# A graph attention on one Trainium2 core: who adds the fourth row of each group

## The chip, the cores and the metric

The kernel runs on one NeuronCore of a Trainium2 chip, as one launch. The metric is the device time of that launch in microseconds, the median of several runs. Everything is float32 here unless said otherwise. Five engines work side by side, each with its own instruction queue: TensorE (PE in the profile) multiplies matrices into PSUM, VectorE (DVE) and ScalarE (ACT) compute elementwise, GpSimd (POOL) issues the gathers, and SyncE (SP) issues plain transfers. They meet through semaphores.

## The reference, cut to what matters

The graph has 1250 nodes of 768 features and 20000 edges. Two graph attentions (GATv2) follow each other, then a relational graph convolution. The second attention has one head and is where the change lies:

```
fs = h @ Wos + bos
fd = h @ Wod + bod
e = leaky_relu(fs[src] + fd[dst], 0.2)        # one row of 768 per edge
logits = sum(e * attn)                         # one number per edge
alpha = softmax of logits over the edges with the same dst
out[dst] = sum over edges of alpha * fs[src]
out = elu(out)
```

The leaky rectifier is split as 0.2 x + 0.8 max(x, 0). The part 0.2 x is linear, so its dot product with attn is worked out once per node and travels as column 768 of the rows of fs and fd. Per edge there remains max(fs + fd, 0) times 0.8 attn, summed over the 768 features.

## The kernel before, in words

Nodes are sorted by their number of edges and put into 10 tiles of 128, one node per partition. A **group** is S = 4 edges of each node of a tile: 4 rows of 776 numbers in each partition. A table says which tile each group belongs to. There are 48 groups, run as a hardware loop of 12 turns with U = 4 groups unrolled in each. The sums are kept in a running softmax: top holds the largest logit so far, den the sum of exponentials, acc the weighted sum of rows, and with every group the old sums are scaled by exp(old top - new top).

The second attention is the function attention_single, from L1110. Who does what for group u:

- **GpSimd** (gather_edges, L790 to L798): copies the place of the node's next record into index, adds one, gathers the record of group u+3 (rec), then gathers the four rows of group u+2 with four indirect transfers. It waits for the sums (summed) of the group that used the row buffer before, and for VectorE's signal read.
- **TensorE**: first the add for group u+2: for each half of 384 columns it multiplies the fourth row (BY_PE = 3) by the identity and then fd by the identity into the same PSUM tile pS (L1201, L1203). Then the weighted sums of group u: four matmuls of two halves with diagonal matrices share as weights, into pA (L1219), and last the old sum acc with share 0 (L1224), once ScalarE has stored acc of the group before (kept). One float32 matmul shows as two records, so a group has 8 records of add, 16 of L1219 and 4 of L1224.
- **VectorE**, for group u: arguments (L1275 to L1287, ten small steps to ex), count (L1292 to L1297), dot of group u+1, weigh (L1303 to L1307). The dot adds fd to rows 0 to 2 into leak (L1253), adds the linear parts (lin, L1256), and runs four multiply-and-sum instructions max(x, 0) * attr with an accumulated sum (L1266): three on leak and the fourth on pS, for which it waits on sum_pe. Before the loop there is the dot of group 0, so 49 dots run, the last of them for a spare group.
- **ScalarE**: exp of ex (L1181), five diagonal matrices share from the identity (L1185), and the copy of pA back to acc for the group before (keep, L1172).

The order on each engine is written out by hand in the program. Nothing is planned by costs. Waits between engines have a slack of one or two groups: the PSUM tiles, dots, lin, ex and share are double, the row buffers fourfold. At the end of the stage all engines meet at a barrier.

Of the kernel before, what the change touches and what calls it, by code (L numbers as in the profile page):

```python
# [4 lines left out]
F32, I32, BF16 = mybir.dt.float32, mybir.dt.int32, mybir.dt.bfloat16  # L5
# [6 lines left out]
P = 128  # L12
# [7 lines left out]
HALF = D // 2  # L20
ROWS_AHEAD = 2
S = 4
U = 4
# [44 lines left out]
def gnn_kernel(nc, io, out):  # L68
    ctx = ExitStack()
    with ctx:  # L70
        taken = {}

        def fresh(name):

            taken[name] = taken.get(name, 0) + 1
            return name if taken[name] == 1 else f"{name}_{taken[name]}"

        def sb(name, shape, dt, where=ctx):
            return where.enter_context(nc.sbuf_tensor(fresh(name), shape, dt))

        def pb(name, shape, dt, where):
            return where.enter_context(nc.psum_tensor(fresh(name), shape, dt))
# [17 lines left out]
        ident = sb("ident", [P, P], F32)  # L100
# [16 lines left out]
        def sems(where, *names):  # L117
            made = [nc.alloc_semaphore(fresh(n)) for n in names]
            where.semaphores += made
            return made  # L120

        @contextmanager
        def stage():

            with ExitStack() as st:
                st.semaphores = []
                yield st
                nc.clear_and_free_semaphores(st.semaphores)
                nc.all_engine_barrier()
# [358 lines left out]
        fdt = sb("fdt", [P, NT + 1, W], F32, fd_ctx)  # L488
# [3 lines left out]
        HB = [(0, 0, HALF), (1, HALF, D)]  # L492

        def halves(psum, rows=P):

            return psum[0:rows, :, 0:HALF]

        def split(ap):
            return ap.rearrange("p (a b) -> p a b", a=2)
# [62 lines left out]
        with stage() as st:  # L562
# [3 lines left out]
            of = [[sb(f"of{w}{b}", [P, W], F32, st) for b in range(2)] for w in range(2)]  # L566
            wt = [sb(f"wt{w}", [P, KC, D], F32, st) for w in range(2)]
            bias = [sb(f"bias{w}", [P, D], F32, st) for w in range(2)]
            attr = sb("attr", [P, D], F32, st)
# [173 lines left out]
        def sum_tiles(eng, tile_from, count, i):  # L743

            tiles = []
            for lo in range(0, count, PACK):
                packed = eng.value_load(tile_of_group[0:1, ds(i * U + (tile_from + TBACK + lo), 1)], min_val=0,
                                        max_val=(1 << 4 * PACK) - 1)
                for k in range(min(PACK, count - lo)):
                    tiles.append(eng.snap((packed >> (4 * k)) & 15).with_bounds(min_val=0, max_val=NT))  # L750
            return tiles
# [91 lines left out]
        def rows_wait(eng, b, i, off):  # L843

            eng.wait_ge(b["row_in"][off % U], i * (16 * S) + 16 * S * (off // U + 1))
# [263 lines left out]

        def attention_single():  # L1110

            BY_PE = S - 1
            with stage() as st:
                b = slot_buffers(st, W)
                row, val = b["row"], b["val"]
# [5 lines left out]
                attr = sb("attr", [P, D], F32, st)  # L1121
                leak = sb("leak", [P, S, D], F32, st)
# [8 lines left out]
                share = [sb(f"share{u}", [P, S + 1, P], F32, st) for u in range(2)]  # L1131
                dsum = sb("dsum", [P, 1], F32, st)
                pA = [pb(f"pA{u}", [P, 2, 512], F32, st) for u in range(2)]
                pS = [pb(f"pS{u}", [P, 2, 512], F32, st) for u in range(2)]
                att_in, dve_step, init_ok = sems(st, "att_in", "dve_step", "init_ok")
                sum_ok = Signal(st, "sum_ok", BY_PE, U, U)
                sum_pe = Signal(st, "sum_pe", 1, U, U)
                logits = Signal(st, "logits", S, U, U)
                lin_ok = Signal(st, "lin_ok", 1, U, U)
                ex_in = Signal(st, "ex_in", 1, U, U)  # L1140
# [2 lines left out]
                summed = Signal(st, "summed", 1, U, U)  # L1143
                total = Signal(st, "total", 1, U, U)
# [4 lines left out]
                def of(ap, tile):  # L1149
                    return ap[:, tile, :] if isinstance(tile, int) else ap[:, ds(tile, 1)].rearrange("p o f -> p (o f)")  # L1150

                with nc.Block() as block:
                    @block.sync
                    def _(sp):
                        sp.dma_start(attr[:], io["L0_gnn_attno"].rearrange("h d -> (h d)").partition_broadcast(P))\
                          .then_inc(att_in, 16)
                        sp.wait_ge(att_in, 16)
# [32 lines left out]

                    @block.tensor
                    def _(pe):
                        for s in (summed, total, sum_pe):
                            s.open(pe)
                        pe.wait_ge(init_ok, 1)

                        def add(i, off, tile):
                            rows_wait(pe, b, i, off)
                            logits.wait(pe, i, off - 2)
                            for q, lo, up in HB:  # L1200
                                pe.matmul(pS[off % 2][:, q, 0:HALF], ident[:], row[off % U][:, BY_PE, lo:up],  # L1201
                                          start=True, stop=False)
                                last = pe.matmul(pS[off % 2][:, q, 0:HALF], ident[:], of(fdt, tile)[:, lo:up],  # L1203
                                                 start=False, stop=True)
                            last.then_inc(sum_pe.sem, 1)

                        add(0, 0, 0)
                        second, = sum_tiles(pe, 1, 1, 0)
                        add(0, 1, second)
                        turns = pe.value_load(ctl[0:1, C_TURNS:C_TURNS + 1], min_val=1, max_val=MAX_TURNS)  # L1210
                        with pe.Fori(0, turns) as i:
                            t = sum_tiles(pe, 0, U + 2, i)
                            for u in range(U):
                                add(i, u + 2, t[u + 2])
                                shared.wait(pe, i, u)
                                kept.wait(pe, i, u - 2)
                                for j in range(S):
                                    for q, lo, up in HB:
                                        last = pe.matmul(pA[u % 2][:, q, 0:HALF], share[u % 2][:, 1 + j, :], row[u][:, j, lo:up],  # L1219
                                                         start=j == 0, stop=False)  # L1220
                                last.then_inc(summed.sem, 1)
                                kept.wait(pe, i, u - 1)
                                for q, lo, up in HB:
                                    last = pe.matmul(pA[u % 2][:, q, 0:HALF], share[u % 2][:, 0, :], of(acc, t[u])[:, lo:up],  # L1224
                                                     start=False, stop=True)
                                last.then_inc(total.sem, 1)

                    @block.vector
                    def _(dve):
# [18 lines left out]
                        def dot(i, off, tile):  # L1248
                            rows_wait(dve, b, i, off)
                            fd = of(fdt, tile)  # L1250
                            for j in range(BY_PE):
                                logits.wait(dve, i, off - 1, j + 1)
                                dve.tensor_tensor(leak[:, j, :], row[off % U][:, j, 0:D], fd[:, 0:D], ALU.add)\  # L1253
                                   .then_inc(sum_ok.sem, 1)
                            lin_ok.wait(dve, i, off - 1)
                            dve.tensor_tensor(lin[off % 2][:], row[off % U][:, :, D:W][:, :, 0],  # L1256
                                              fd[:, D:D + 1].to_broadcast([P, S]), ALU.add).then_inc(lin_ok.sem, 1)
                            for j in range(S):
                                if j < BY_PE:
                                    sum_ok.wait(dve, i, off, j + 1)  # L1260
                                    ins = dict(out=leak[:, j, :], in0=leak[:, j, :], in1=attr[:])
                                else:
                                    logits.wait(dve, i, off - 1, j + 1)
                                    sum_pe.wait(dve, i, off)
                                    ins = dict(out=split(leak[:, j, :]), in0=halves(pS[off % 2]), in1=split(attr[:]))
                                dve.scalar_tensor_tensor(scalar=0.0, op0=ALU.max, op1=ALU.mult, **ins,  # L1266
                                                         accum_out=dots[off % 2][:, j, :]).then_inc(logits.sem, 1)

# [43 lines left out]
                        with dve.Fori(0, turns) as i:  # L1312
                            t = sum_tiles(dve, 0, U + 1, i)
# [331 lines left out]

        settle(True)
        attention_single()
        settle(False)

# [221 lines left out]
        with stage() as st:  # L1871
            b = slot_buffers(st, D)
# [276 lines left out]
```

## Time and profile before

| | us |
|---|---|
| median of 3 runs | 3903.91 |
| lowest and highest of them | 3902.19, 3904.19 |
| the profiled execution, its time | 3898.73 |
| the profiled execution, its span | 3897.1 |
| second attention in it, first to last work | 1262 to 1762 |

The profile is of one execution of its own. Its span runs from the first to the last instruction, and 1.6 us of its time lie around it. In the rows, PE is the matmul part of TensorE and PEld its loads of weights; PEclk is the share of the full clock granted to TensorE, where 0.50 is 1.2 GHz and 1.00 is 2.4 GHz. Ends of matmuls are modelled, so the records overlap. An idle time is followed by what ended it; "issue" is time for which the profile shows no releaser. L with a number is a line of the program.

### The profile page before, as it was taken

How to read it: one execution, taken by the hardware profiler on the slowest of the kernel's cores; microseconds unless marked ns; L12 is line 12 of the kernel's file. 1: busy time of each engine (PE TensorE's matmuls, PEld its weight loads, DVE VectorE, ACT ScalarE, POOL GpSimd, SP SyncE). 2: the span in 40 equal slices, each digit the busy share in tenths (PEclk: the TensorE clock that was granted, in tenths of full speed). 3: DMA queues.
4: the chain of work that ended last, by engine and by line, in shares of the span. 5: the costliest groups of instructions: out<-in, count | busy, mean ns of one | idle time of the engine just before them, and what ended most of it. 6: DMA issues, size and time to landing. Idle time of an engine off the chain costs nothing. (4 is left out here: it accounts for less than half of the span.)

```text
span 3897.1 us, 63629 instructions
## 1 busy us (share of the span) xinstructions
PE 3095.4 (79%) x14356; PEld 2355.9 (60%) x14357; DVE 2506.5 (64%) x5040; ACT 1734.7 (45%) x5380; POOL 1494.4 (38%) x1783
## 2 busy tenths in 40 slices
PE   0196788888697999994779999999999964444699
PEld 0053444444354555552369999999999964444455
DVE  8233889898666888885645554455545549999412
ACT  0010788888621222222324444444444428888400
POOL 0373545454355666661111111111111137777200
PEclk9998899999898999997889999999999986666799
DMA  0233444343454555552155555555555545555300
GB/s 26 79 86 107 136 127 129 117 128 118 147 182 141 163 155 158 157 154 81 44 187 186 180 177 180 183 182 179 176 186 182 184 134 170 176 174 174 128 9 32
DMA packets 181911, 546.64 MB, mean 140 GB/s; under 512 B 37415, under 2 KB 82299, under 8 KB 181563
## 3 DMA queue, kind: packets, MB, share of 16 engines
q0 software_dynamic: 77264, 331.42, 27.7%
q1 hardware_dynamic: 53772, 143.14, 11.9%
q10 hardware_dynamic: 50832, 71.59, 5.1%
q8 instruction: 17, 0.28, 0.0%
q14 instruction: 26, 0.21, 0.0%
HBM read 428.42 MB, written 117.91 MB: 140 GB/s over the span
## 5 line engine op out<-in xcount | busy, mean ns | idle before, releaser
L1804 PE MATMUL pO<-wh,gT 128*128 128x384 f32 x4128 | 1094.5, 339 | 4.5 <-DVE wl L1842 4.5
L1804 PEld LDWEIGHTS pO<-wh,gT 128*128 128x128 f32 x4128 | 750.7, 188 | 5.3 <-DVE wl L1842 5.3
L1804 PE MATMUL pO<-wl,gT 128*128 128x384 f32 x2064 | 691.8, 335 | 0.0
L798 POOL DMA_INDIRECT row<-fs_d,rec x400 | 439.6, 1099 | 351.4 <-PE pA L986 187.7
L1828 DVE TENSOR_SCALAR cntge<-pT 128x768 int32<-128x768 int32 x173 | 165.7, 958 | 571.2 <-PE pT L504 570.3
L511 PE MATMUL pO<-wt,hT 128*128 128x384 f32 (+1 forms) x1200 | 420.0, 512 | 42.5 <-ACT hT L1510 19.6
L1756 ACT ACTIVATE gT<-cntge 128x256 fp32r<-128x256 f32 x1038 | 371.7, 410 | 170.5 <-PE pO L1804 121.4
L1766 ACT ACTIVATE nrow<-pO 128x384 f32<-128x384 f32 x344 | 165.9, 482 | 542.1 <-PE pO L1804 542.1
L1804 PEld LDWEIGHTS pO<-wl,gT 128*128 128x128 f32 x2064 | 389.1, 189 | 0.0
L1936 PE MATMUL pC<-identb,own 128*128 128x128 bf16 x960 | 192.9, 304 | 235.0 <-ACT cntge L1917 121.2
L511 PEld LDWEIGHTS pO<-wt,hT 128*128 128x128 f32 (+1 forms) x1200 | 236.8, 200 | 215.9 <-issue 68.7
L924 ACT ACTIVATE sj<-sj 128x96 f32<-128x96 f32 x1176 | 313.1, 268 | 99.7 <-DVE sj L1041 99.7
L1726 POOL DMA_INDIRECT g<-hr_d,gindex x173 | 167.5, 968 | 379.0 <-PE pT L504 373.3
L963 PE MATMUL pS<-row,ident 128*128 128x384 f32 x400 | 184.1, 545 | 128.3 <-DVE sj L1041 89.5
L1737 POOL COPY gindex<-source 128x1 int32 x172 | 43.5, 253 | 614.0 <-DMA g<-hr_d,gindex 614.0
L1936 PEld LDWEIGHTS pC<-identb,own 128*128 128x128 bf16 x960 | 114.2, 143 | 245.4 <-issue 75.6
L1219 PE MATMUL pA<-row,share 128*128 128x384 f32 x768 | 255.8, 486 | 0.0
L986 PE MATMUL pA<-row,ident 128*128 128x384 f32 x768 | 255.5, 486 | 0.0
L798 POOL DMA_INDIRECT row<-y_d,rec x200 | 211.2, 1056 | 66.6 <-issue 61.3
L1914 ACT ACTIVATE far<-nrow,source 128x1280 bf16<-128x1280 f32 x144 | 196.2, 1362 | 83.2 <-DVEq L1989 80.1
L924 ACT ACTIVATION_READ_ACCUMULATOR sj<-sj 128x1 f32 x1176 | 219.7, 187 | 0.0
L1219 PEld LDWEIGHTS pA<-row,share 128*128 128x128 f32 x768 | 146.4, 191 | 102.6 <-issue 1.5
(336 smaller groups left out, 5689.8 us busy)
## 6 DMA issues: line engine op xcount, KB each, us to landing
raw<-in_L_gnn_W_rel_dram SPq DMA_DIRECT2D x204, 384.0 KB
y_d<-nrow ACTq DMA_DIRECT2D x344, 192.0 KB
y_d<-nothing SPq DMA_DIRECT2D x53, 384.0 KB
row<-fs_d,rec POOLq DMA_INDIRECT x400, 4.5
kept_d<-fdt ACTq DMA_DIRECT2D x1, 3840.0 KB, 15.7
kept<-kept_d SPq DMA_DIRECT2D x1, 3840.0 KB
fs_d<-of SPq DMA_DIRECT2D x9, 388.0 KB
fd_d<-of SPq DMA_DIRECT2D x9, 388.0 KB, 2.6
```

Source lines behind the costliest of these rows:

```text
L511: last = pe.matmul(dst[0:rows, q, 0:HALF], rows_t[:, c * P:c * P + rows], w[:, c, lo:up], start=c == 0, stop=c == KC - 1)
L798: pool.indirect_dma_start(b["row"][u][:, j, :], None, table, bass.IndirectOffsetOnAxis(ap=b["rec"][u][:, 2 * j + field:2 * j + field + 1], ...
L924: last = act.activation(of_head, of_head, ACT.Copy, accum_out=dots[off % U][:, j, h:h + 1])
L963: pe.matmul(pS[j][:, q, 0:HALF], ident[:], row[off % U][:, S // 2 + j, lo:up], start=True, stop=False)
L986: last = pe.matmul(pA[:, q, 0:HALF], share, row[u][:, j, lo:up], start=j == 0, stop=j == S - 1)
L1219: last = pe.matmul(pA[u % 2][:, q, 0:HALF], share[u % 2][:, 1 + j, :], row[u][:, j, lo:up], start=j == 0, stop=False)
L1726: pool.indirect_dma_start(g[:], None, hr_d, bass.IndirectOffsetOnAxis(ap=gindex[:], axis=0))\
L1756: act.activation(gT[:, c].bitcast(F32R), cut[:, :, c * P:(c + 1) * P], ACT.Copy).then_inc(gT_ok.sem, 1)
L1766: act.activation(y[:, lo:up], pO[:, q, 0:HALF], ACT.Copy).then_inc(evac_ok.sem, 1)
L1804: last = pe.matmul(pO[:, q, 0:HALF], gT[:, c, half, :].bitcast(F32R), w[:, c, lo:up].bitcast(F32R), start=c == 0 and k == 0, stop=c == KC ...
L1914: act.activation(far[:], of_node[:], ACT.Square, bias=source[u % 2][:, j:j + 1], scale=-1.0)\
L1936: last = pe.matmul(pC[u % 2][:, c // 4, (c % 4) * P:(c % 4 + 1) * P], equal[u % 2][j][:, c * P:(c + 1) * P], identb[:], start=j == 0, stop ...
```

## The change

VectorE adds fd to all four rows of a group. TensorE's add, its PSUM tiles pS and the signal sum_pe are gone. TensorE keeps the weighted sums and the scaled old sum. The fourth multiply-and-sum of VectorE now reads leak, as the other three do.

```diff
--- before.py
+++ after.py
@@ -1109,7 +1109,6 @@
 
         def attention_single():
 
-            BY_PE = S - 1
             with stage() as st:
                 b = slot_buffers(st, W)
                 row, val = b["row"], b["val"]
@@ -1131,10 +1130,8 @@
                 share = [sb(f"share{u}", [P, S + 1, P], F32, st) for u in range(2)]
                 dsum = sb("dsum", [P, 1], F32, st)
                 pA = [pb(f"pA{u}", [P, 2, 512], F32, st) for u in range(2)]
-                pS = [pb(f"pS{u}", [P, 2, 512], F32, st) for u in range(2)]
                 att_in, dve_step, init_ok = sems(st, "att_in", "dve_step", "init_ok")
-                sum_ok = Signal(st, "sum_ok", BY_PE, U, U)
-                sum_pe = Signal(st, "sum_pe", 1, U, U)
+                sum_ok = Signal(st, "sum_ok", S, U, U)
                 logits = Signal(st, "logits", S, U, U)
                 lin_ok = Signal(st, "lin_ok", 1, U, U)
                 ex_in = Signal(st, "ex_in", 1, U, U)
@@ -1190,28 +1187,15 @@
 
                     @block.tensor
                     def _(pe):
-                        for s in (summed, total, sum_pe):
+                        for s in (summed, total):
                             s.open(pe)
                         pe.wait_ge(init_ok, 1)
 
-                        def add(i, off, tile):
-                            rows_wait(pe, b, i, off)
-                            logits.wait(pe, i, off - 2)
-                            for q, lo, up in HB:
-                                pe.matmul(pS[off % 2][:, q, 0:HALF], ident[:], row[off % U][:, BY_PE, lo:up],
-                                          start=True, stop=False)
-                                last = pe.matmul(pS[off % 2][:, q, 0:HALF], ident[:], of(fdt, tile)[:, lo:up],
-                                                 start=False, stop=True)
-                            last.then_inc(sum_pe.sem, 1)
-
-                        add(0, 0, 0)
-                        second, = sum_tiles(pe, 1, 1, 0)
-                        add(0, 1, second)
                         turns = pe.value_load(ctl[0:1, C_TURNS:C_TURNS + 1], min_val=1, max_val=MAX_TURNS)
                         with pe.Fori(0, turns) as i:
-                            t = sum_tiles(pe, 0, U + 2, i)
+                            t = sum_tiles(pe, 0, U, i)
                             for u in range(U):
-                                add(i, u + 2, t[u + 2])
+                                rows_wait(pe, b, i, u)
                                 shared.wait(pe, i, u)
                                 kept.wait(pe, i, u - 2)
                                 for j in range(S):
@@ -1248,7 +1232,7 @@
                         def dot(i, off, tile):
                             rows_wait(dve, b, i, off)
                             fd = of(fdt, tile)
-                            for j in range(BY_PE):
+                            for j in range(S):
                                 logits.wait(dve, i, off - 1, j + 1)
                                 dve.tensor_tensor(leak[:, j, :], row[off % U][:, j, 0:D], fd[:, 0:D], ALU.add)\
                                    .then_inc(sum_ok.sem, 1)
@@ -1256,13 +1240,8 @@
                             dve.tensor_tensor(lin[off % 2][:], row[off % U][:, :, D:W][:, :, 0],
                                               fd[:, D:D + 1].to_broadcast([P, S]), ALU.add).then_inc(lin_ok.sem, 1)
                             for j in range(S):
-                                if j < BY_PE:
-                                    sum_ok.wait(dve, i, off, j + 1)
-                                    ins = dict(out=leak[:, j, :], in0=leak[:, j, :], in1=attr[:])
-                                else:
-                                    logits.wait(dve, i, off - 1, j + 1)
-                                    sum_pe.wait(dve, i, off)
-                                    ins = dict(out=split(leak[:, j, :]), in0=halves(pS[off % 2]), in1=split(attr[:]))
+                                sum_ok.wait(dve, i, off, j + 1)
+                                ins = dict(out=leak[:, j, :], in0=leak[:, j, :], in1=attr[:])
                                 dve.scalar_tensor_tensor(scalar=0.0, op0=ALU.max, op1=ALU.mult, **ins,
                                                          accum_out=dots[off % 2][:, j, :]).then_inc(logits.sem, 1)
```

## Rows read from the trace of the kernel before

**Rows 1.** The page: busy us (share of the span) xinstructions of each engine.
```profile
PE 3095.4 (79%) x14356; PEld 2355.9 (60%) x14357; DVE 2506.5 (64%) x5040; ACT 1734.7 (45%) x5380; POOL 1494.4 (38%) x1783
```

**Rows 2.** Windows, the stage: PE, PEld, DVE, ACT, POOL busy (x), PEclk, DMA, GB/s.
```profile
1262.00:1762.00 500.00, 461.07 (x1360) 261.27 (x1360) 427.88 (x1357) 137.87 (x349) 317.96 (x338) 0.97 0.51 156
```

**Rows 3.** Timeline, two groups: start us, us, engine, line, op [idle before <-releaser].
```profile
1502.21 0.23 DVE L1275 TENSOR_SCALAR val<-slot,left 128x4 f32<-128x4 f32 x1 [0.15 <-issue]
...
1504.65 0.18 POOL L790 COPY index<-next 128x1 int32 x1 [1.37 <-DVEq L1293]
...
1505.28 2.69 DVE L1253 TENSOR_TENSOR leak<-row,fdt 128x768 f32<-128x768 f32 x3 [0.15 <-issue]
...
1507.89 0.16 DVE L1256 TENSOR_TENSOR lin<-row,fdt 128x4 f32<-128x4 f32 x1
...
1509.09 1.52 POOL L798 DMA_INDIRECT row<-fs_d,rec  x1 [0.30 <-issue]
...
1509.72 0.95 DVE L1266 SCALAR_TENSOR_TENSOR leak<-leak,attr 128x768 f32<-128x768 f32 x1
1509.79 5.32 PE L1219 MATMUL pA<-row,share 128*128 128x384 f32 x16
...
1510.60 0.95 DVE L1266 SCALAR_TENSOR_TENSOR leak<-pS,attr 128x768 f32<-128x768 f32 x1
...
1512.17 0.94 POOL L798 DMA_INDIRECT row<-fs_d,rec  x1 [0.30 <-issue]
1513.40 0.23 DVE L1275 TENSOR_SCALAR val<-slot,left 128x4 f32<-128x4 f32 x1 [1.51 <-issue]
...
1523.24 0.23 DVE L1275 TENSOR_SCALAR val<-slot,left 128x4 f32<-128x4 f32 x1 [0.15 <-issue]
```

**Rows 4.** Waits of VectorE in the stage: us in total, times, longest us.
```profile
DVE val L1275 <- issue: 21.0, 39, 1.6
DVE ge L1295 <- DVE place_f L1292: 7.1, 46, 0.2
```

**Rows 5.** TensorE's waits; lines L1201, L1203, L798: count, duration ns min/median/max, starts.
```profile
PE pS L1201 <- DMA row<-fs_d,rec: 31.4, 33, 2.5
...
L1201 PE MATMUL pS<-row,ident x200: 486/486/1009, 1262.4 to 1753.2; 128*128 128x384 f32 x100
...
L1203 PE MATMUL pS<-fdt,ident x200: 486/486/848, 1263.9 to 1753.8; 128*128 x98, 128*128 128x384 f32 x2
...
L798 POOL DMA_INDIRECT row<-fs_d,rec x178: 942/948/1686, 1290.3 to 1735.7; - x178
```

**Rows 6.** Tile leak: operation, count, duration ns min/median/max, first and last start.
```profile
L1253 DVE TENSOR_TENSOR leak<-row,fdt x147: 948/951/960, 1262.5 to 1750.1; 128x768 f32<-128x768 f32 x147
...
L1266 DVE SCALAR_TENSOR_TENSOR leak<-pS,attr x49: 946/951/953, 1267.9 to 1753.7; 128x768 f32<-128x768 f32 x49
```

**Rows 7.** Timeline of the stage's end.
```profile
1747.41 1.57 ACT L1185 ACTIVATE share<-ident,pe 128x128 f32<-128x128 f32 x5
...
1753.82 5.03 PEld L1219 LDWEIGHTS pA<-row,share 128*128 128x128 f32 x16
...
1754.83 0.16 DVE L1307 TENSOR_TENSOR den<-den,dsum 128x1 f32 x1
...
1760.95 0.81 ACT L1172 ACTIVATE acc<-pA 128x768 f32 x1 [8.85 <-PE pA L1224]
```

**Rows 8.** Timeline of TensorE in the first attention, after an idle gap.
```profile
754.78 1.48 PE L963 MATMUL pS<-row,ident 128*128 128x384 f32 x2 [2.02 <-DVE sj L1041]
756.05 1.49 PE L965 MATMUL pS<-fdt,ident 128*128 x2
...
758.51 0.81 PE L965 MATMUL pS<-fdt,ident 128*128 x2
```

**Rows 9.** Late in the kernel: a gap (timeline), a burst between gaps (windows).
```profile
3331.21 0.39 PE L1936 MATMUL pC<-identb,own 128*128 128x128 bf16 x2 [5.27 <-ACT cntge L1917]
...
3313.00:3318.00 5.00, 4.45 (x40) 4.18 (x40) 4.33 (x13) 4.04 (x4) 3.82 (x4) 0.50 0.52 147
```

## Prediction

> **What bounds the kernel now.** The page comes first, to see that no engine is full over the whole span: TensorE is busy for 79% of it and VectorE for 64% [rows 1]. That says nothing about this change, because it touches one stage of many. The view of windows, cut to the second attention (its first TensorE and VectorE work begins at 1262, its last ScalarE copy ends at 1762), gives 461 us of TensorE and 428 us of VectorE in 500 us, at a granted clock of 0.97 [rows 2]. Both look nearly full, so busy shares cannot tell which sets the pace. TensorE's share is also modelled, since pipelined matmuls overlap.
>
> The timeline of two groups tells more [rows 3]. VectorE goes from one group's first instruction to the next in 9.84 us, or 11.19 us where a turn of four groups ends (1502.21, 1513.40, 1523.24). Inside a group it runs three adds, the small lin, four multiply-and-sum instructions and the small softmax steps, with gaps of 0.15 us. The long gap, 1.51 us, stands only where the loop turns.
>
> Who ends VectorE's idle time is in the view of waits: its largest entry is 21.0 us in 39 pieces put down to issue, the next is a wait on VectorE's own result, the smaller ones are of these two kinds, and no entry names TensorE [rows 4]. TensorE does wait: 31.4 us in 33 pieces for gathered rows, always at the identity matmul of the add [rows 5]. I read this as: **VectorE sets the pace, TensorE has a little room.** The add for group u+2 was issued two groups ahead, so its result always lies ready: in the timeline the multiply-and-sum on pS starts 0.88 us after the one before it, as the others do [rows 3].
>
> **The change, part by part.**
>
> *Added on VectorE.* One more row add per group. There are 147 of three per dot, so 49 dots (48 groups and one spare at the end), each lasting 951 ns in the median [rows 6]. Lasting is not pitch: three adds take from 1505.28 to 1507.89, when the next instruction starts, 0.87 us each [rows 3]. I take 0.875, halfway to the 0.88 pitch of the multiply-and-sum. That is 48 x 0.875 = 42.0 us before the last group's softmax arguments are ready, and 49 x 0.875 = 42.9 us for VectorE's own end. All of it lies on the path, since VectorE has nothing but its own order in front of it. The bounds are 0.87 (41.8 us for 48) and the whole duration 0.951 (45.6 us).
>
> *Moved source.* The fourth multiply-and-sum reads leak from SBUF and no longer pS from PSUM: the one on pS lasts 951 ns in the median [rows 6], the one on leak 0.95 us in the timeline, both with a pitch of 0.88 [rows 3], so nothing. The Trainium skill ("VectorE: DVE Perf Modes", section on the errata that SBUF sources pay a fixed extra latency) gives 58 cycles of fixed cost to an SBUF source and 120 to a PSUM source at 0.96 GHz, which would make this step 65 ns cheaper, 3.2 us over 49; the sum by it would be 34.9 us where mine is 38. The trace does not show that difference, and I follow the trace.
>
> *Waits.* The added add waits for the fourth logit of the group before, which VectorE finished itself long ago; the wait on sum_pe goes. Behind both stand only VectorE's own instructions. Nothing.
>
> *Removed on TensorE.* 200 + 200 records of matmul (pS from row and from fdt), eight per group [rows 5]. At the pitch of 5.32 us for 16, or about 0.324 [rows 3], that is 2.6 us per group. TensorE is not the pace setter, so it gains nothing inside the loop. Its wait for rows of group u+2 goes too; the wait that it gets instead, for rows of group u, is long met, because VectorE's dot of that group already needed them.
>
> *Gained at the end.* Now the shares of the last group are ready at 1747.41 + 1.57 = 1748.98, but TensorE first finishes older work and makes one more useless add, and loads the first share at 1753.82. From there to the last copy of acc it is 7.94 us (1761.76) [rows 7]. Afterwards TensorE stands idle when the shares come: 1748.98 + 42.0 + 0.1 + 7.9 = 1799.0. VectorE's own end, 1754.83 + 0.16 + 42.9 = 1797.9, comes earlier. So the stage ends 37.2 us later, not 42.9.
>
> *GpSimd.* Its row gathers take 0.94 us beside small VectorE work (at 1512.17) and 1.52 us beside wide VectorE work on SBUF (at 1509.09) [rows 3]. VectorE gets 1.75 us more of such work per group, so two gathers may become slow, +1.1 us. From index to the end of the fourth gather is 8.5 us now (1504.65 to 1512.17 + 0.94), so 9.6 afterwards, in a period of 11.0 (the mean of three groups at 9.84 and one at 11.19, plus 0.875). Its rows are needed two dots later. Hidden; if the cover were gone, each microsecond over 11.0 would cost 48 us. The queues of SP and ScalarE get and lose nothing; ScalarE works 137.87 / 48 = 2.9 us per group [rows 2].
>
> *Clock at the end.* The last burst may start at the lower clock (see the rival). Where it fell, about six records ran at the lower pitch of 0.64 before it rose [rows 8], 6 x 0.32 = 1.9 us; I take half, 1 us. The far bound is all 20 records, +6.4 us.
>
> **Sum:** 37.2 + 1 = +38 us on the profiled execution, 3898.7 (span 3897.1 and 1.6 around it) to 3937. The median of the runs shown is 5.2 us above that execution, so 3942.
>
> **Rivals.**
>
> *The clock makes TensorE the bound.* TensorE's group becomes a burst of 20 records, 6.8 us (5.32 and 1.45 as they follow each other), then idle for about 4.2 of 11.0 us. In the first attention the clock had fallen after a gap of 2.02 us: pairs of records took 1.27 us from start to start instead of 0.65, but after 3.7 us of work it was back [rows 8]. Late in the kernel, a gap is 5.27 us and a burst between two gaps has 4.45 us of work at a granted 0.50, the lower clock throughout [rows 9]. If a whole burst stayed there, 20 x 0.64 + 0.6 for the two starts = 13.4 us would exceed the 11.0 of VectorE, and through kept, ex_ok and the gathers everybody would fall in step: 48 x 2.4 = 115 us more, 4057 us. The Trainium skill ("TensorE: Matmul & The Clock Gate", HAM oscillation) states that a loop whose bursts are parted by idle waits goes back to the lower clock and starts every burst cold, which speaks against this change. For the rival: gap as in [rows 9]. Against: a burst longer than that one, and the quick return in [rows 8]; also it limits itself, as a slow burst leaves a short gap. Chance 5%.
>
> *TensorE set the pace already, so the kernel gets faster.* The place is sum_pe and the gathers that wait for summed. VectorE is idle for 493 - 428 = 65 us from 1262 to its end near 1755, 1.35 us per group. If those gaps were really waits on TensorE, they would vanish with its 2.6 us per group, and the added 0.875 would fit: 42.9 - 65 = -22 us, 3882. It decides from 0.875 us of waiting per group on. For it: TensorE's 461 busy us. Against: the gaps are all 0.15 us or at loop turns, and none is ended by TensorE [rows 4]. Chance 2%; a partial case, where about the added time is absorbed (3900 to 3911), 3%.
>
> *GpSimd's gathers become the bound.* If the two fast gathers took the worst 1.69 us instead of 0.95 [rows 5], the chain would be 8.5 + 1.5 = 10.0 us, still under 11.0. Only if the two others and the record's gather grew as well, by 1.5 us together, would it show, 0.5 us per group, 24 us, 3966. For it: one gather in the stage did take 1.69. Against: the median is 0.948. Chance 3%.
>
> **How the numbers follow.** The forecast has the other 87%. Its own range takes the add at 0.87 to 0.951, the end at -3 to +6 us and about 2 us for the run: 3936 to 3953. The other cases hold 13%, so the range that should hold 8 in 10 is this one. A measurement of this kernel can tell some 0.2%, 7.8 us, from no change. Faster by more than that: 2%. Within: 3%. Slower: 95%, the forecast and the two slow rivals.
>
> **What would show it.** Right: 196 adds instead of 147, group to group 10.7 and 12.1 us on VectorE with unchanged gaps, stage about 38 us longer, TensorE's idle time ended by ScalarE's shares, no matmul on pS, and other stages unmoved. The clock in the stage may fall below 0.97 without cost. Wrong: VectorE waits that name ex or rows, groups of 13 us (clock), a VectorE period that stays at 9.84 (TensorE was the bound), or adds longer than 951 ns.

## The result, and the profile after

| | before | changed |
|---|---|---|
| median of 4 runs, us | 3903.05 | 3937.89 |
| lowest and highest | 3900.49, 3904.19 | 3935.66, 3939.36 |
| time and span of the profiled execution | 3898.73, 3897.1 | 3939.36, 3937.7 |
| clock granted to TensorE in it, mean of the span | 0.916 | 0.878 |

The ratio is 1.009 (95% interval 1.0072 to 1.0107), 34.8 us slower by the medians. The forecast was 3942, slower by 38, with a range of 3936 to 3953; the median lies 2 us above the lower end of it.

The view of windows over the stage of the changed kernel (us; busy and count of PE, PEld, DVE, ACT, POOL; PEclk, DMA share, GB/s), which answers to [rows 2]:

```profile
1262.00:1800.00 538.00, 381.39 (x960) 207.33 (x960) 470.11 (x1406) 135.45 (x349) 342.33 (x339) 0.84 0.51 145
```

VectorE is busy for 470 us where it was 428. TensorE is busy for 381 us where it was 461, though its granted clock is down from 0.97 to 0.84. The views of the tiles leak and share and of the gather line (count, duration ns min/median/max, first and last start) answer to [rows 5, 6]:

```profile
L1237 DVE TENSOR_TENSOR leak<-row,fdt x196: 947/951/961, 1262.4 to 1792.9; 128x768 f32<-128x768 f32 x196
L1245 DVE SCALAR_TENSOR_TENSOR leak<-leak,attr x196: 947/951/955, 1266.0 to 1796.4; 128x768 f32<-128x768 f32 x196
...
L1203 PE MATMUL pA<-row,share x768: 486/486/1008, 1275.1 to 1795.9; 128*128 128x384 f32 x192
...
L798 POOL DMA_INDIRECT row<-fs_d,rec x178: 942/1398/1517, 1289.3 to 1776.3; - x178
```

There are 49 more adds (196 instead of 147), each lasting 951 ns as before. All 196 multiply-and-sum instructions read leak now and last 951 ns in the median. The median gather takes 1398 ns instead of 948.

Two groups in the timeline, as [rows 3]:

```profile
1501.32 0.23 DVE L1254 TENSOR_SCALAR val<-slot,left 128x4 f32<-128x4 f32 x1 [0.19 <-issue]
...
1504.30 3.56 DVE L1237 TENSOR_TENSOR leak<-row,fdt 128x768 f32<-128x768 f32 x4
...
1505.04 5.43 PE L1203 MATMUL pA<-row,share 128*128 128x384 f32 x16 [1.19 <-ACT share L1182]
...
1507.78 0.15 DVE L1240 TENSOR_TENSOR lin<-row,fdt 128x4 f32<-128x4 f32 x1
...
1509.93 1.45 POOL L798 DMA_INDIRECT row<-fs_d,rec  x1 [0.30 <-issue]
...
1511.97 0.23 DVE L1254 TENSOR_SCALAR val<-slot,left 128x4 f32<-128x4 f32 x1 [0.19 <-issue]
...
1515.68 7.12 PE L1203 MATMUL pA<-row,share 128*128 128x384 f32 x16 [3.93 <-ACT share L1182]
...
1522.62 0.23 DVE L1254 TENSOR_SCALAR val<-slot,left 128x4 f32<-128x4 f32 x1 [0.19 <-issue]
```

Read VectorE first: 1501.32, 1511.97, 1522.62, so 10.65 us per group; where a turn ends it is 12.04 (to 1534.66). The mean period over the stage is (1787.2 - 1270.0) / 47 = 11.00 us, against (1745.3 - 1269.7) / 47 = 10.12 before, from the first and the last start of val. Four adds take from 1504.30 to 1507.78, 0.87 us each. Only the gap ahead of val is 0.19 us instead of 0.15. Then TensorE: its sums for one group start at 1505.04 after 1.19 us of idleness and take 5.43 us; those for the next start at 1515.68 after 3.93 us of idleness, and the same 16 records take 7.12 us. VectorE's period does not notice. TensorE's timeline shows the longest burst of the stage and one from its middle, then one turn of four groups, as they repeat from 1600 on, and the last two bursts:

```profile
1451.58 8.44 PE L1203 MATMUL pA<-row,share 128*128 128x384 f32 x16 [6.71 <-ACT share L1182]
...
1526.33 5.43 PE L1203 MATMUL pA<-row,share 128*128 128x384 f32 x16 [2.23 <-ACT share L1182]
...
1603.87 7.12 PE L1203 MATMUL pA<-row,share 128*128 128x384 f32 x16 [3.93 <-ACT share L1182]
...
1614.52 7.12 PE L1203 MATMUL pA<-row,share 128*128 128x384 f32 x16 [2.23 <-ACT share L1182]
...
1627.96 7.31 PE L1203 MATMUL pA<-row,share 128*128 128x384 f32 x16 [5.03 <-ACT share L1182]
...
1637.33 5.43 PE L1203 MATMUL pA<-row,share 128*128 128x384 f32 x16 [0.77 <-ACT share L1182]
...
1780.27 7.95 PE L1203 MATMUL pA<-row,share 128*128 128x384 f32 x16 [3.93 <-ACT share L1182]
...
1790.91 5.43 PE L1203 MATMUL pA<-row,share 128*128 128x384 f32 x16 [1.41 <-ACT share L1182]
```

In the turn shown, the bursts after gaps of 2.23, 3.93 and 5.03 us take 7.1 to 7.3 us, three of the four; the one after 0.77, and the last of the stage after 1.41, take 5.43. The gap alone does not decide: the burst at 1526.33 has the same gap of 2.23 as the one at 1614.52 and takes 5.43, not 7.12. Of the stage's 48 bursts 29 take over 5.5 us, and none stays slow to its end: 16 records at the lower pitch of 0.64 would be 10.2 us, the longest is 8.44.

The view of waits, 1290 to 1780, says who waits (us in total, times, longest), against [rows 4, 5]:

```profile
PE pA L1203 <- ACT share L1182: 135.7, 40, 6.8
...
DVE val L1254 <- issue: 23.3, 45, 1.6
...
DVE ge L1274 <- DVE place_f L1271: 6.9, 45, 0.2
```

TensorE no longer waits for gathered rows but for ScalarE's shares, which wait for VectorE. VectorE's list has issue and its own results, as before. The end of the stage answers to [rows 7]; its last row is the first transfer of the stage that follows:

```profile
1789.29 1.57 ACT L1182 ACTIVATE share<-ident,pe 128x128 f32<-128x128 f32 x5
...
1790.91 4.81 PEld L1203 LDWEIGHTS pA<-row,share 128*128 128x128 f32 x16 [2.02 <-ACT share L1182]
...
1797.57 0.16 DVE L1286 TENSOR_TENSOR den<-den,dsum 128x1 f32 x1
1797.82 0.81 ACT L1169 ACTIVATE acc<-pA 128x768 f32 x1 [6.27 <-PE pA L1208]
1799.50 0.34 SPq L1384 DMA_DIRECT2D lnw<-in_L_gnn_lno_w_dram  x1
```

And the same first transfer in the kernel before, with the product of the relation stage further on (first and last start):

```profile
1762.64 0.34 SPq L1405 DMA_DIRECT2D lnw<-in_L_gnn_lno_w_dram  x1
...
L1804 PE MATMUL pO<-wh,gT x4128: 333/334/686, 1978.5 to 3177.2; 128*128 128x384 f32 x197
```

The same product in the changed kernel:

```profile
L1783 PE MATMUL pO<-wh,gT x4128: 334/334/686, 2016.1 to 3218.1; 128*128 128x384 f32 x197
```

The stage that was changed ends 1799.50 - 1762.64 = **36.9 us** later; its first add starts at 1262.4 in one kernel and 1262.5 in the other. From there to the first product the two kernels differ by 0.7 us. The product's stage itself lasts 1202.0 us instead of 1198.7, which makes the profiled executions 40.6 us apart. That stage was not touched. In the ten kernels tried below it lasts 1197.9 us in one (run 9) and 1201.5 to 1202.6 in the nine others, without relation to what was changed, and I take the 3.3 us for scatter. So the profiled execution of the kernel before was a short one, which fits its 3898.7 under a median of 3903.

### The profile page after: what moved, and what is told of

The parts are those of the page before. It is cut to its first block and busy times, and to the rows that moved or that the text cites. A ratio compares the mean times of both kernels' runs of the same rounds, so it can differ in the third digit from the quotient of the medians.

```text
span 3937.7 us, 62628 instructions
## 1 busy us (share of the span) xinstructions
PE 3017.4 (77%) x13956; PEld 2304.4 (59%) x13957; DVE 2549.7 (65%) x5089; ACT 1732.8 (44%) x5380; POOL 1524.3 (39%) x1783
## 5 line engine op out<-in xcount | busy, mean ns | idle before, releaser
L798 POOL DMA_INDIRECT row<-fs_d,rec x400 | 465.3, 1163 | 344.9 <-PE pA L986 187.7
L1203 PE MATMUL pA<-row,share 128*128 128x384 f32 x768 | 319.9, 579 | 173.1 <-ACT share L1182 173.0
L511 PE MATMUL pO<-wt,hT 128*128 128x384 f32 (+1 forms) x1200 | 417.5, 510 | 41.9 <-ACT hT L1489 19.6
L1203 PEld LDWEIGHTS pA<-row,share 128*128 128x128 f32 x768 | 170.9, 228 | 321.7 <-issue 160.3
L798 POOL DMA_INDIRECT row<-y_d,rec x200 | 210.8, 1054 | 66.6 <-issue 61.3
```

The lines of the kernel that those rows point to most:

```text
L511: last = pe.matmul(dst[0:rows, q, 0:HALF], rows_t[:, c * P:c * P + rows], w[:, c, lo:up], start=c == 0, stop=c == KC - 1)
L798: pool.indirect_dma_start(b["row"][u][:, j, :], None, table, bass.IndirectOffsetOnAxis(ap=b["rec"][u][:, 2 * j + field:2 * j + field + 1], ...
```

## The experiments

All are timed against the kernel before on the same chip in the same rounds, so the ratios are compared, not the bare times: the kernel before itself read 3902.1, 3902.5 and 3898.5 in the three sets (runs 1 to 4, 5 to 8, 9 and 10). Where the length of the stage is compared, it is taken from VectorE's first row add to the first transfer of the next stage. The diffs are cut to the lines that matter; where the number of adds changes, the counts of their signals change with it.

**1. Three adds, none on TensorE** (the changed kernel; fd is left out of the fourth row).

```diff
-for j in range(S):
+for j in range(S - 1):
     dve.tensor_tensor(leak[:, j, :], row[off % U][:, j, 0:D], fd[:, 0:D], ALU.add)
...
-ins = dict(out=leak[:, j, :], in0=leak[:, j, :], in1=attr[:])
+src = leak[:, j, :] if j < S - 1 else row[off % U][:, j, 0:D]
+ins = dict(out=leak[:, j, :], in0=src, in1=attr[:])
```

> The changed kernel with the fourth add of VectorE left out: fd is not added to the fourth row, whose multiply-and-sum reads the gathered row itself. TensorE has no add either. If VectorE sets the pace, the group takes the 10.1 us of the kernel before, since the same three adds are left, TensorE idles more than in either kernel and its clock falls, and only the end of the stage is 5 us shorter (no add ahead of the last sums): about 3898 us. If TensorE's adds had set the pace, VectorE's gaps vanish and the time is near 3880. If the lower clock by itself cost anything, the time is above 3903.

Measured: ratio 0.9996 (0.9986 to 1.0005), 3901.1 us. Windows of the stage, the instruction that writes val, and the row gathers from 1290 to 1780 (count, ns min/median/max):

```profile
1262.00:1740.00 478.00, 348.45 (x919) 191.92 (x920) 412.50 (x1305) 130.65 (x334) 339.97 (x332) 0.87 0.55 159
...
L1258 DVE TENSOR_SCALAR val<-slot,left x48: 228/266/398, 1271.3 to 1749.4; 128x4 f32<-128x4 f32 x48
...
L798 POOL DMA_INDIRECT row<-fs_d,rec x184: 942/1395/1701, 1290.0 to 1750.0; - x184
```

TensorE's add is gone here too, 348 us of work instead of 441 in the same window, and nothing is gained: the mean period of VectorE, (1749.4 - 1271.3) / 47, is 10.17 us against 10.12. TensorE did not set the pace. Of the 5 us expected at the end, the end gave them (9.0 us from the start of the last share to the next stage, 14.0 before). Period and a stage begun 2 us later took them back. The period's part has a trace: val lasts 266 ns in the median instead of 229 and up to 398, an instruction that had never varied (228 to 231 in the kernel before). No view names what stretches it, so that stays open.

**2. Both adds: VectorE's fourth, and TensorE's, whose sum is not read** (an edit of the kernel before).

```diff
-for j in range(BY_PE):
+for j in range(S):
     dve.tensor_tensor(leak[:, j, :], row[off % U][:, j, 0:D], fd[:, 0:D], ALU.add)
...
-    sum_pe.wait(dve, i, off)
-    ins = dict(out=split(leak[:, j, :]), in0=halves(pS[off % 2]), in1=split(attr[:]))
+if j == S - 1:
+    sum_pe.wait(dve, i, off)
+sum_ok.wait(dve, i, off, j + 1)
+ins = dict(out=leak[:, j, :], in0=leak[:, j, :], in1=attr[:])
```

> The kernel before with the fourth add on VectorE as well; TensorE's add stays and nobody reads its result. VectorE's theory: the period is VectorE's 11.0 us, as in the changed kernel; TensorE's 9.1 us of work fit into it, its clock stays near 1.0, and the last sums no longer queue behind anything: about 3940, as the changed kernel. If the lower clock of the changed kernel costs time there, this one is faster than the changed kernel by more than 3 us. If taking work from TensorE had given time back, this one is slower than the changed kernel by more than 5 us.

Measured: ratio 1.0102 (1.0085 to 1.0119), 3941.8 us. Windows, and TensorE's wait from 1262 to 1800 (the longest, 19.4, lies ahead of the stage's first work):

```profile
1262.00:1740.00 478.00, 411.10 (x1203) 231.83 (x1204) 420.54 (x1254) 121.44 (x312) 311.50 (x309) 0.96 0.51 148
...
PE pS L1201 <- DMA row<-fs_d,rec: 91.1, 40, 19.4
```

With TensorE's work kept, its clock is 0.96, and the kernel is no faster than the changed one with 0.84. VectorE's mean period, from the first to the last val, is (1786.9 - 1271.5) / 47 = 10.97 us against (1787.2 - 1270.0) / 47 = 11.00, so the lower clock can have cost at most 0.04 us per group, 1.8 in the stage, as long as the add that TensorE keeps costs the loop nothing itself (run 1 shows nothing gained without it). TensorE's lost work gives nothing back inside the loop. In the trace it is 12.4 us from the last share to the next stage against 9.0 in the changed kernel: the add ahead of the last sums waited for the rows of the spare group. The expectation that this delay would vanish was wrong, and it is most of the 4 us between the two medians.

**3. Five adds.**

```diff
-for j in range(S):
+for j in range(S + 1):
...
+dve.tensor_tensor(leak[:, j, :], row[off % U][:, j % S, 0:D], fd[:, 0:D], ALU.add)
```

> The changed kernel with a fifth add on VectorE, of a row already added, into a tile of its own that nobody reads. VectorE's theory: another 49 x 0.886 = 43 us, 3981. If part of an add is hidden behind something else, less; a theory by which four adds just fill a slack would give less for the fourth than for the fifth.

Measured: ratio 1.0211 (1.0194 to 1.0228), 3985.0 us, 47 us over the changed kernel. VectorE's mean period is 11.90 us, 0.90 over the changed kernel's 11.00, where the fourth add had cost 0.88: each add costs its pitch of 0.87 in full and the fourth filled no slack. The stage is 44.3 us longer than the changed kernel's, where 43 were expected; val has a median of 264 ns and a longest of 400 here as well.

**4. TensorE's add made twice in the kernel before.**

```diff
-for q, lo, up in HB:
+for q, lo, up in HB + HB:
     pe.matmul(pS[off % 2][:, q, 0:HALF], ident[:], row[off % U][:, BY_PE, lo:up],
               start=True, stop=False)
```

> The kernel before with TensorE's add made twice (the second pass overwrites the first with the same sums), 36 records instead of 28 per group. If VectorE sets the pace before, TensorE's 11.7 us of records and 0.3 to 0.6 us of starts now exceed 10.1: 48 x (12.0 to 12.3 - 10.1) = +88 to +103, 3991 to 4006. If TensorE set the pace already, its whole 2.6 us per group come on top: +125, 4028.

Measured: ratio 1.0182 (1.0165 to 1.0199), 3973.2 us. Timeline of TensorE, and VectorE's new wait:

```profile
1501.47 5.32 PE L1219 MATMUL pA<-row,share 128*128 128x384 f32 x16
...
1513.08 5.32 PE L1219 MATMUL pA<-row,share 128*128 128x384 f32 x16
...
DVE leak L1266 <- PE pS L1203: 40.3, 34, 1.8
```

Now TensorE is the bound: 11.61 us from sums to sums, 36 records of 0.3225 without a gap, and VectorE waits for pS. The time, +71 us, lies below both expectations, +88 to +103 and +125. The first had added 0.3 to 0.6 us per group for starts, which vanish when the engine is never idle: 48 x (11.61 - 10.12) = 72 us, and the stage ends 72.4 us later. The second, by which TensorE set the pace before, is out. The kernel before stood at 28 x 0.3225 = 9.03 us of TensorE under 10.12 of VectorE. TensorE had 1.1 us of room per group, not the 2.6 of another row.

**5. One wide add in the kernel before.**

```diff
-for j in range(BY_PE):
-    dve.tensor_tensor(leak[:, j, :], row[off % U][:, j, 0:D], fd[:, 0:D], ALU.add)
+dve.tensor_tensor(leak[:, 0:BY_PE, :], row[off % U][:, 0:BY_PE, 0:D], over(fd[:, 0:D], 1, [P, BY_PE, D]), ALU.add)
```

> The kernel before with VectorE's three adds of a group made as one instruction of 3 x 768 elements, fd repeated over the rows. Three adds now take 2.61 us from start to next start, 0.87 each, of which 768 elements at the slope of the other wide work are about 0.80. VectorE's theory: 2 x 0.07 = 0.14 us less per group, 49 groups, -7: 3895. If VectorE's length did not set the time before, no change from 3902.

Measured: ratio 0.9992 (0.9983 to 1.0001), 3898.6 us: not settled against no change, and half of what was expected. Timeline, and the gather of records (ns min/median/max):

```profile
1505.97 2.56 DVE L1252 TENSOR_TENSOR leak<-row,fdt 128x2304 f32<-128x2304 f32 x1 [0.27 <-issue]
1508.45 0.16 DVE L1255 TENSOR_TENSOR lin<-row,fdt 128x4 f32<-128x4 f32 x1
...
L793 POOL DMA_INDIRECT rec<-by_dst_d,index x46: 984/3012/3148, 1288.8 to 1738.5; - x46
```

The add's pitch is 2.48 us, the 0.13 under 2.61 that was expected. But the mean period fell by 0.04 only (10.08, by the starts of val): the first multiply-and-sum now waits for the whole wide add, 0.11 us behind lin instead of 0.07, and the gap ahead of the add is 0.27 us in this group where it was 0.15. I had not thought of GpSimd: the record gather issued beside the wide add lasts 3.0 us, against 1.4.

**6. One wide add in the changed kernel.**

```diff
-for j in range(S):
-    logits.wait(dve, i, off - 1, j + 1)
-    dve.tensor_tensor(leak[:, j, :], row[off % U][:, j, 0:D], fd[:, 0:D], ALU.add).then_inc(sum_ok.sem, 1)
+logits.wait(dve, i, off - 1)
+dve.tensor_tensor(leak[:], row[off % U][:, :, 0:D], over(fd[:, 0:D], 1, [P, S, D]), ALU.add).then_inc(sum_ok.sem, 1)
```

> The changed kernel with its four adds as one instruction of 4 x 768 elements. VectorE's theory: 3 x 0.07 = 0.21 us less per group, -10 from 3938: 3928. It stays slower than the kernel before by 25, since a row's elements cost VectorE 0.80 us wherever they stand. If a long instruction holds GpSimd's gathers up so far that rows come late, VectorE waits on rows and the gain is smaller.

Measured: ratio 1.0084 (1.0070 to 1.0098), 3934.4 us. Timeline of a group, and the stage's end:

```profile
1502.83 3.36 DVE L1236 TENSOR_TENSOR leak<-row,fdt 128x3072 f32<-128x3072 f32 x1
...
1502.91 4.10 POOL L798 DMA_INDIRECT row<-fs_d,rec  x1 [0.30 <-issue]
...
1506.22 0.96 DVE L1244 SCALAR_TENSOR_TENSOR leak<-leak,attr 128x768 f32<-128x768 f32 x1
...
1792.31 0.81 ACT L1169 ACTIVATE acc<-pA 128x768 f32 x1 [6.27 <-PE pA L1208]
1798.20 0.34 SPq L1383 DMA_DIRECT2D lnw<-in_L_gnn_lno_w_dram  x1
```

3928 was expected. The mean period fell by 0.15 us to 10.85 where 0.21 was expected, 7 us over the stage, and 4 of them are lost again at its end. A row gather issued 0.08 us behind the wide add lasts 4.10 us and ends after it; about one of a group's four does so. That cost VectorE nothing, since the rows are needed two groups later. At the end, 5.1 us pass between the last copy's end at 1793.12 and the next stage, where the changed kernel has 0.9. The profile names no engine or transfer for that, and it stays open.

**7. TensorE's add behind the sums, in the kernel before.**

```diff
-add(i, u + 2, t[u + 2])
 shared.wait(pe, i, u)
...
 last.then_inc(total.sem, 1)
+add(i, u + 2, t[u + 2])
```

> The kernel before with only the order on TensorE changed: its add for group u+2 behind the sums of group u. Inside the loop nothing, since VectorE sets the pace; TensorE's waits for gathered rows go. At the end of the stage the last copy of acc comes 5 us sooner after the shares, the useless add behind it gives about 1.5 back: -3 to -4, 3899. If the wait for rows ahead of the sums had cost time inside the loop, more than 10 us are gained.

Measured: ratio 0.9990 (0.9981 to 0.9999), 3899.0 us. Timeline of the end:

```profile
1748.68 1.57 ACT L1185 ACTIVATE share<-ident,pe 128x128 f32<-128x128 f32 x5
...
1751.21 5.32 PE L1218 MATMUL pA<-row,share 128*128 128x384 f32 x16
...
1758.02 0.81 ACT L1172 ACTIVATE acc<-pA 128x768 f32 x1 [7.08 <-PE pA L1223]
...
1759.60 0.81 PE L1203 MATMUL pS<-fdt,ident 128*128 x2
...
1761.31 0.34 SPq L1405 DMA_DIRECT2D lnw<-in_L_gnn_lno_w_dram  x1
```

The period stays 10.12, and TensorE waits for shares instead of rows. From the start of the last shares to the next stage it is 12.6 us; the kernel before needed 15.2 (1747.41 in [rows 7] to 1762.64). The stage itself is 2.2 us shorter, and the ratio says -0.1%, a little less than expected and at the edge of what these runs can tell.

**8. Both of these together** (wide add of three rows, add behind the sums).

```diff
-dve.tensor_tensor(leak[:, j, :], row[off % U][:, j, 0:D], fd[:, 0:D], ALU.add)
+dve.tensor_tensor(leak[:, 0:BY_PE, :], row[off % U][:, 0:BY_PE, 0:D], over(fd[:, 0:D], 1, [P, BY_PE, D]), ALU.add)
...
-add(i, u + 2, t[u + 2])
...
+add(i, u + 2, t[u + 2])
```

> The kernel before with the one wide add of three rows, and TensorE's add for group u+2 issued behind the sums of group u instead of ahead of them. Both gains should add: -7 for the wide add, and -3 to -4 at the end of the stage, where the last sums start as soon as the shares are there and only one useless add of 2.6 us stands behind them: 3892. That would be faster than both kernels.

Measured: ratio 0.9990 (0.9981 to 0.9999), 3897.4 us. Half of the expected gain. In its profiled execution the stage is 5.8 us shorter than the kernel before's, with a mean period of 10.07. It beats the changed kernel by 1% and the kernel before by 0.1%, which is at the edge of what these runs can tell.

**9 and 10. A small step moved to GpSimd**, in the changed kernel (9) and in the kernel before with the order of run 7 (10).

```diff
-v.mark(dve.tensor_tensor(into, into, ge[:].rearrange("p s r -> p (s r)"), ALU.add))
+v.mark(pool.tensor_tensor(into, into, ge[off % 2][:].rearrange("p s r -> p (s r)"), ALU.add))
```

The tile ge is doubled for it, and VectorE signals GpSimd when ge is written.

> The changed kernel with one small step of VectorE moved to GpSimd: the add of ge to cntge, 140 numbers per partition, once per group, behind the row gathers; ge is double. VectorE's theory: from the start of that add to the next start are 0.46 us, which leave VectorE's path: 48 x 0.46 = 22 us less than 3938, 3916, as long as GpSimd's chain (9.1 us of gathers and copies with four slow gathers, and 0.5 us for the add) stays under VectorE's 10.5 us. If GpSimd's add and VectorE's wide work shut each other out, the add waits for VectorE or VectorE's work stretches, and the gain is under 15 us.

> The kernel before with the same step on GpSimd, and TensorE's add behind the sums as in the run that changed the order alone. VectorE's group falls to 9.66 us, TensorE's 28 records of 0.3225 us are 9.03 us with 0.3 to 0.6 for starts, so both fit: 22 + 3.5 us less than 3902, 3877, faster than both kernels. If TensorE is the bound from 9.4 us on, the same; if it needs more than 9.7, up to 5 us of the gain are missing. If the fourth add had stayed on VectorE (the run beside this), the gap between the two is again 38 to 40 us.

Measured: (9) ratio 1.0088 (1.0074 to 1.0101), 3932.6 us; (10) ratio 0.9995 (0.9986 to 1.0004), 3896.9 us. Of 22 us nearly nothing came, although GpSimd never became the bound. Timeline of a group of run 10, its adds (ns min/median/max), and the groups of the adds in runs 10 and 9 from 1290 to 1740 (busy us, mean ns):

```profile
1504.18 3.19 DVE L1276 TENSOR_TENSOR leak<-row,fdt 128x768 f32<-128x768 f32 x3
...
1505.17 0.50 POOL L1177 TENSOR_TENSOR cntge<-cntge,ge 128x140 f32 x1
...
1507.29 0.15 DVE L1279 TENSOR_TENSOR lin<-row,fdt 128x4 f32<-128x4 f32 x1
...
L1276 DVE TENSOR_TENSOR leak<-row,fdt x147: 944/959/1378, 1263.0 to 1750.3; 128x768 f32<-128x768 f32 x147
...
L1276 DVE TENSOR_TENSOR leak<-row,fdt 128x768 f32<-128x768 f32 x134 | 140.1, 1099 | 4.7 <-issue 1.3
...
L1260 DVE TENSOR_TENSOR leak<-row,fdt 128x768 f32<-128x768 f32 x164 | 157.6, 1019 | 2.0
```

Three adds that took 2.69 us end to end [rows 3] take 3.19, with a 0.50 us add of GpSimd beside them; single adds last up to 1378 ns. Over the stage an add of run 10 lasts 1099 ns in the mean, where it was 953: three of them lose 0.44 us per group, as much as the step of 0.46 had cost VectorE. In run 9 four adds lose 4 x (1019 - 952) ns = 0.27 us, and the step that writes ge, 468 ns instead of 304, another 0.16. The mean period is 10.119 us in run 10, that of the kernel before, and 10.92 in run 9, against 11.00. The last reading of run 9's expectation, that the two shut each other out and the gain stays under 15 us, holds. The two runs are 35.7 us apart, where 38 to 40 were expected: the price of the fourth add once more.

## Why the prediction was right

- **VectorE sets the pace.** Shown from both sides: with TensorE's add gone and three adds on VectorE the time is that of the kernel before (run 1, ratio 0.9986 to 1.0005), and keeping it beside VectorE's fourth add leaves the loop within 0.04 us per group of the changed kernel's (run 2).
- **The price of an add.** Predicted 0.875 us per group. Pitch measured: 0.87. The mean period rose from 10.12 to 11.00, 0.885; the gap ahead of val, 0.19 instead of 0.15 in the groups shown, is part of it. To the last shares, predicted 42.0 us; measured 1789.29 - 1747.41 = 41.9.
- **The gain at the end.** Predicted 37.2 us for the stage; measured 36.9. The last copy ends at 1798.63 where 1799.0 was worked out. VectorE's end, worked out as 1797.9, is 1797.73.
- **Clock at the end.** The 1 us taken for a slow last burst was not needed: the last sums came after a gap of 1.41 us and ran in 5.43, the full clock. The burst before them took 7.95 after 3.93, so the term had no sure value; without it the sum would have been 37, nearer to what was measured. Its size was fair: a burst of 7.12 us is 1.7 longer than one of 5.43, where 1.9 had been read.
- **The moved source.** Nothing was predicted and nothing is seen, 951 ns both times. The Trainium skill's figures for the two sources ("VectorE: DVE Perf Modes", section on the errata) would have given 3.2 us back; the trace does not show them. The 34.9 us of the sum by them lies next to the 34.8 of the medians, but that is chance: not one of the 196 lasts under 947 ns, and the stage grew by 36.9.
- **GpSimd.** The gathers grew and stayed hidden, as predicted: one more of the shown group at 1.45 us, where two were allowed for, and the median from 948 to 1398 ns. It was not the fourth add that did it: with three adds the median is 1395 ns as well (run 1), and with TensorE's add kept it is 1399 (run 2). What the three kernels share is the moved source, a fourth multiply-and-sum that reads SBUF only. It matters where the gathers fall beside that step: in run 9, where they start at another point of the group, the median is 947. In the kernel before, a gather started beside the one on pS (1510.60 in [rows 3]) is not lengthened:

```profile
1510.91 0.95 POOL L798 DMA_INDIRECT row<-fs_d,rec  x1 [0.30 <-issue]
```

- **The clock rival.** Its first half came true: bursts after gaps, and a clock of 0.84. Its second did not: the mean of an L1203 record rose from 486 to 579 ns, and TensorE still had 173 us of waiting for shares in the stage. No burst stayed slow throughout, which the rival needed, and a slow burst only shortens its own gap. The rule of the Trainium skill ("TensorE: Matmul & The Clock Gate", HAM oscillation), that idle waits between bursts bring the lower clock back, agrees here with 29 of 48 bursts; the other 19 ran at full clock, so that not every burst starts cold. It is worth next to nothing in time, since TensorE is not the bound: run 2 bounds it at 1.8 us.
- **TensorE as the bound already.** It was not: with 9.03 us of work per group it had 1.1 us of room, and run 4 shows what it looks like when the work, 11.61 us, exceeds VectorE's 10.12: VectorE waits for pS.
- The sum, 38, stands against 34.8 by the medians and 36.9 in the stage. The difference between these two is within the scatter of the untouched stages. Of the 4 us between forecast and median, 3.2 are this sum and 0.9 the median of the kernel before, which was 3903.9 on record and 3903.05 in this comparison.

## What to carry to other kernels

When two engines look equally full, ask whose idle time is ended by the other, not who is busier; then a step moved onto the pace setter costs its pitch (start to next start, 0.87 us here), not its duration (0.95). Work that is moved off an engine with slack brings back only what its queue delays at the ends of the stage, here 5 us of 126 (49 adds of 8 x 0.3225). A lower clock on an engine that waits anyway cost at most 1.8 us here, and work sent to GpSimd beside two-input VectorE instructions is not free to VectorE.

## What the runs showed of the hardware that was not expected

- VectorE and GpSimd hold each other up. A GpSimd add of 140 numbers (0.50 us) lengthened VectorE's row adds beside it, 2.69 to 3.19 us for three (run 10). The other way, a gather that GpSimd issued 0.08 us after a 3.36 us add took 4.10 us, and a record gather beside a 2.56 us add took 3.0 us instead of 1.4 (runs 6, 5). The Trainium skill ("SBUF — State Buffer", Who interferes with whom) states that a VectorE instruction with two SBUF inputs contends with a GpSimd instruction that reads SBUF. The two-way stretching agrees, and so do the gathers beside multiply-and-sum instructions: 0.95 us beside the one with a source in PSUM, 1.45 to 1.52 beside those with both in SBUF. The page takes the gathers' issue to escape beside a tensor_tensor, by an inference; these rows speak against that.
- The idle gap before a burst did not decide its clock. In the changed kernel TensorE ran bursts of 7.12 us and of 5.43 us after the same gap of 2.23 us, and in run 1 full ones after gaps of up to 3.38 us; all after 3.8 us or more had a slow stretch, and all ended at full clock.
